# Two layers on one core: five PSUM banks for the exponentials behind the last maximum, and the second layer's routing steps placed later

## The reference, cut to what matters

```
x  = L0_attn_x                                  # (2, 1024, 128)
xn = layernorm(x);  s = attention(xn) @ WO;  g = silu(ffn0(xn));  x = x + s * g
xn = layernorm(x);  s = recurrent(xn);       g = silu(ffn1(xn));  x = x + s * g

attention:  score = Q K^T / sqrt(8) + causal mask;  exp(score - max) / sum;  times V
ffn1:       logits = x @ router_w;  raw = softmax(logits)
            idx1 = argmax(raw);  idx2 = argmax(raw without idx1)
            place of a token in its expert = exclusive count of the tokens before it in the group
            combine/dispatch by one-hot(place) ... expert -> gelu(x w0) * (x w1) -> wo
```

## Time and profile before

| | |
|---|---|
| median of three runs | 617.03 us |
| profiled execution, its own time | 616.33 us |
| its span, first to last instruction | 614.5 us |
| PE busy | 573.1 us (93%) |
| DVE busy | 476.7 us (78%) |
| ACT busy | 330.9 us (54%) |
| POOL busy | 190.4 us (31%) |
| mean granted TensorE clock | 0.981 |

### The profile page before, as it was taken

How to read it: one execution, slowest core, us unless ns; L and a number is a source line. 1 busy time by engine, 2 the same in 40 slices (tenths; PEclk the granted TensorE clock), 3 DMA queues, 4 the chain that set the end, 5 groups by cost and what they waited for, 6 DMA issues and landing times.

```text
span 614.5 us, 11961 instructions
## 1 busy us (share of the span) xinstructions
PE 573.1 (93%) x3901; PEld 352.2 (57%) x3902; DVE 476.7 (78%) x1307; ACT 330.9 (54%) x602; POOL 190.4 (31%) x221
## 2 busy tenths in 40 slices
PE   2878999999999999899999998989899999999996
PEld 1433544444444534899999963535446665656554
DVE  6799889999989898455555578666899899976465
ACT  2762567676777776555555558864223642362224
POOL 1451000000254452133333310000007685688300
PEclk9898899999999999999999999999999999999999
DMA  8955727070813171211111034215011322421412
GB/s 185 210 182 206 241 77 216 3 217 1 224 31 109 53 226 20 56 49 47 47 47 47 26 97 128 71 41 151 0 46 25 97 59 54 130 79 40 126 42 68
DMA packets 55612, 57.99 MB, mean 94 GB/s; under 512 B 8651, under 2 KB 39403, under 8 KB 55515
## 3 DMA queue, kind: packets, MB, share of 16 engines
q1 hardware_dynamic: 51242, 50.56, 29.9%
q0 software_dynamic: 4320, 6.81, 3.5%
HBM read 41.96 MB, written 18.85 MB: 99 GB/s over the span
## 4 chain that ended last, share of the span: by engine, by line
PE 76%; DVE 16%; ACT 4%; issue 2%; DMA 1%; SPq 1%; ACTq 0%; DVEq 0%
PE banks L1689 11%; PE banks L1831 10%; PE banks L1756 8%; PE banks L1778 7%; PE banks L1964 7%; PE banks L1701 6%; PE banks L1953 5%; PE banks L1950 5%; PE banks L2015 4%; DVE banks L1239 4%; DVE mpart L1242 3%; PE banks L1759 2%; ACT arena L809 1%; PE banks L1840 1%; PE banks L1598 1%
## 5 line engine op out<-in xcount | busy, mean ns | idle before, releaser
L809 ACT ACTIVATE arena<-banks 128x512 f32<-128x512 f32 (+1 forms) x304 | 154.3, 583 | 75.1 <-PE banks L1759 40.7
L1239 DVE CUSTOM_DVE_ANT_0 banks<-banks,arena 128x512 f32<-128x512 f32 (+3 forms) x256 | 119.7, 511 | 9.2 <-PE banks L1778 8.3
L1756 PE MATMUL banks<-arena 128*128 128x512 bf16 (+3 forms) x384 | 116.6, 331 | 4.0 <-ACT arena L809 2.8
L1778 PE MATMUL banks<-arena 96*128 96x512 bf16 (+3 forms) x384 | 113.5, 336 | 4.8 <-DVE mpart L1239 2.7
L1242 DVE TENSOR_REDUCE mpart<-banks 128x1 f32<-128x512 f32 x128 | 85.8, 683 | 9.1 <-PE banks L1778 8.1
L1689 PE MATMUL banks<-arena 128*128 128x128 f32 x624 | 76.3, 275 | 1.0 <-ACT arena L743 1.0
L1689 PEld LDWEIGHTS banks<-arena 128*128 128x128 f32 x624 | 72.8, 192 | 1.5 <-ACT arena L743 1.5
L1831 PE MATMUL banks<-arena 128*9 128x512 f32 (+3 forms) x768 | 70.7, 487 | 0.0
L851 ACT ACTIVATE arena<-banks 125x512 f32<-125x512 f32 (+2 forms) x48 | 28.4, 595 | 71.2 <-PE banks L1950 46.2
L1756 PEld LDWEIGHTS banks<-arena 128*128 128x128 bf16 x384 | 37.8, 99 | 49.6 <-issue 23.8
L620 POOL DMA_INDIRECT results<-arena x39 | 37.7, 967 | 77.4 <-DVE arena L1133 77.4
(11 more groups left out here) (295 smaller groups left out, 858.0 us busy)
## 6 DMA issues: line engine op xcount, KB each, us to landing
k_parts<-arena SPq DMA_DIRECT2D x6, 768.0 KB, 8.1
arena<-in_L_ffn_experts_w_dram SPq DMA_DIRECT2D x2, 2048.0 KB, 11.1
arena<-results SPq DMA_DIRECT2D x8, 512.0 KB, 6.6
arena<-k_parts SPq DMA_DIRECT2D x7, 576.0 KB
arena<-q_parts SPq DMA_DIRECT2D x28, 144.0 KB
arena<-in_L_ffn_w_kernel_dram SPq DMA_DIRECT2D x8, 344.0 KB, 3.8
slots<-in_pad_rows_dram SPq DMA_DIRECT2D x1, 2535.0 KB, 12.3
arena<-slots SPq DMA_DIRECT2D x39, 65.0 KB, 1.8
```

Of the source, the lines that this page charges most:

```text
L809: act.activation(Pr[:, r % 4, heads[0]:heads[-1] + 1, 0:n], ring_e[e % 3][:, 0:len(heads) * n].rearrange("p (j c) -> p j c", j=len(heads)) ...
L1239: ins = dve.tensor_tensor_reduce(unmasked, unmasked, tail_mask[:, 512 - n:512], 1.0, -BIG, ALU.add, ALU.max, part[:, at:at + 1])
L1756: ins = pe.matmul(ring_e[e % 3][:, at * n:at * n + n], QK[:, slot, j, 1, P * kt:P * kt + P], QK[:, slot, j, 0, q:q + n], start=True, stop= ...
L1778: ins = pe.matmul(ps[:, at * n:at * n + n], QK[0:TALL, slot, j, 0, P * i:P * i + P], QK[0:TALL, slot, j, 1, 512 * half:512 * half + n], st ...
```

## The change

Two things change, both for group 7 and the end of group 6.

First, from the last maximum on (it is the unit of group 7's head 3, tile 5, in group 6) the seven ring banks are dealt out anew: 0, 1, 2, 5 and 6 to the exponentials, 3 and 4 to the small units. A function that walks the step list takes for each step the bank used longest ago among those allowed, and notes which semaphore count says that the bank's last content has been read. The engines then wait for that count.

Second, `MIDDLE` puts the steps of layer 1 later: the two `x_turn` from keys 39 and 41 to 48 and 50, `logits1` and `route_max` from 45 and 46 to 54, `route_exp` and `scale` from 49 to 53, `route_choice` from 50 to 54, `places1` and `route_places` from 56 and 57 to 64.

```diff
-          28: [("norm", 0)], 30: [("norm", 1)], 39: [("x_turn", 0)], 41: [("x_turn", 1)], 45: [("logits1",)], 46: [("route_max",)], 49: [("route_exp",), ("scale",)], 50: [("route_choice",)], 56: [("places1",)], 57: [("route_places",)]}
+          28: [("norm", 0)], 30: [("norm", 1)], 48: [("x_turn", 0)], 50: [("x_turn", 1)], 53: [("route_exp",), ("scale",)],
+          54: [("logits1",), ("route_max",), ("route_choice",)], 64: [("places1",), ("route_places",)]}
...
+E_BANKS, M_BANKS = (0, 1, 2), (3, 4, 5, 6)
+E_BANKS_LAST, M_BANKS_LAST = (0, 1, 2, 5, 6), (3, 4)
...
+    last_maximum = max(n for n, step in enumerate(steps) if step[0] == "p1")
+    def take(banks, n, freed):
+        bank = min(banks, key=lambda i: (used[i], i))
+        before, used[bank], held[bank] = held[bank], n, freed
+        return bank, before
+    for n, step in enumerate(steps):
+        e_banks, m_banks = (E_BANKS, M_BANKS) if n < last_maximum else (E_BANKS_LAST, M_BANKS_LAST)
...
             def unit_free():
-                if unit >= 4:
-                    name, n = FREES[unit - 4]
+                if M_AFTER[unit] is not None:
+                    name, n = M_AFTER[unit]
                     pe.wait_ge(Z[name], n)
-                return ring_m[unit % 4]
+                return banks[:, M_BANK[unit], :]
...
-                        if e >= 3:
-                            pe.wait_ge(Z["e_free"], e - 2)
+                        if E_AFTER[e] is not None:
+                            name, freed = E_AFTER[e]
+                            pe.wait_ge(Z[name], freed)
```

More of the change, by code:

```diff
@@ L211 @@
 RING_STEPS = ("p1", "logits", "counts", "maxrow", "turn", "attn_turn", "attn_out", "x_turn", "places1", "logits1")
+E_BANKS, M_BANKS = (0, 1, 2), (3, 4, 5, 6)
+E_BANKS_LAST, M_BANKS_LAST = (0, 1, 2, 5, 6), (3, 4)
 def ring_tables():
     frees, unit_of, reads_before, reads = [], {}, {}, 0
[L218 to L221, removed]
+    e_bank, e_after, m_bank, m_after = [], [], [], []
+    steps = [step for k in range(-1, NG + 1) for step in PLANS[k]]
+    last_maximum = max(n for n, step in enumerate(steps) if step[0] == "p1")
+    used, held = dict.fromkeys(E_BANKS + M_BANKS, -1), dict.fromkeys(E_BANKS + M_BANKS)
+    def take(banks, n, freed):
[4 more added lines that the diff above has]
+        e_banks, m_banks = (E_BANKS, M_BANKS) if n < last_maximum else (E_BANKS_LAST, M_BANKS_LAST)
+        if step[0] == "exp":
+            bank, before = take(e_banks, n, ("e_free", len(e_bank) + 1))
+            e_bank.append(bank)
+            e_after.append(before)
+        elif step[0] in RING_STEPS:
+            unit_of[step] = len(frees)
             if step[0] == "maxrow":
                 frees.append(("mrow_ready", 2 * step[1] + step[2] + 1))
-            elif step[0] in RING_STEPS:
+            else:
                 reads += 1
                 frees.append(("m_free", reads))
[L227 to L232, removed]
+            bank, before = take(m_banks, n, frees[-1])
+            m_bank.append(bank)
+            m_after.append(before)
+        elif step[0] in ("negmax", "experts0"):
+            reads_before[step] = reads
+    return frees, unit_of, reads_before, reads, e_bank, e_after, m_bank, m_after
+FREES, UNIT_OF, READS_BEFORE, READS, E_BANK, E_AFTER, M_BANK, M_AFTER = ring_tables()
 def build(nc, x, WQ, WK, WV, WO, gate, w1, w2, w3, WomT, b_om, log_scale, gamma, beta, W1T, b1, W2T, b2,
@@ L358, in build @@
         psO = banks[:, 6:8, :].rearrange("p a c -> p (a c)")
-        ring_e = [banks[:, i, :] for i in range(3)]
-        ring_m = [banks[:, 3 + i, :] for i in range(4)]
         O = banks[:, 7, :]
@@ L800, in _ @@
                             act.wait_ge(mrow_in[half], 16 * (g - 1))
-                        act.copy(mrow[0:3 * HG, g % 2, 512 * half:512 * half + 512], ring_m[unit % 4][0:3 * HG, :]).then_inc(Z["mrow_ready"], 1)
+                        act.copy(mrow[0:3 * HG, g % 2, 512 * half:512 * half + 512], banks[0:3 * HG, M_BANK[unit], :]).then_inc(Z["mrow_ready"], 1)
                     elif step[0] == "exp":
@@ L809, in _ @@
                         act.activation(Pr[:, r % 4, heads[0]:heads[-1] + 1, 0:n],
-                                       ring_e[e % 3][:, 0:len(heads) * n].rearrange("p (j c) -> p j c", j=len(heads)), ACT.Exp,
+                                       banks[:, E_BANK[e], 0:len(heads) * n].rearrange("p (j c) -> p j c", j=len(heads)), ACT.Exp,
                                        scale=SCALE).then_inc(Z["e_free"], 1)
@@ L1752, in _ @@
                             pe.wait_ge(mrow_in[half], 16 * (k + 1))
-                        if e >= 3:
-                            pe.wait_ge(Z["e_free"], e - 2)
+                        if E_AFTER[e] is not None:
+                            name, freed = E_AFTER[e]
+                            pe.wait_ge(Z[name], freed)
                         for at, j in enumerate(heads):
-                            ins = pe.matmul(ring_e[e % 3][:, at * n:at * n + n], QK[:, slot, j, 1, P * kt:P * kt + P],
+                            ins = pe.matmul(banks[:, E_BANK[e], at * n:at * n + n], QK[:, slot, j, 1, P * kt:P * kt + P],
                                             QK[:, slot, j, 0, q:q + n], start=True, stop=kt // 4 != half)
                             if kt // 4 == half:
-                                ins = pe.matmul(ring_e[e % 3][:, at * n:at * n + P], upper_b, ident_b, start=False, stop=True)
+                                ins = pe.matmul(banks[:, E_BANK[e], at * n:at * n + P], upper_b, ident_b, start=False, stop=True)
                         ins.then_inc(Z["e_ready"], 1)
```

## The result

The changed kernel took 619.31 us (median of ten runs, 616.95 to 621.93), the kernel before 617.1 us (median of ten, 614.8 to 619.24). The ratio is 1.0046, with a 95% interval of 1.0029 to 1.0063: slower by 2.8 us (1.8 to 3.9), and clear of noise; the two medians lie 2.2 apart. The forecast was 617.4 with a range up to 618.9; the measured 619.31 lies outside. The profiled execution has a span of 617.4 us against 614.5.

The account below looks back on a forecast made before the run. Bound: PE (76% of the span), through the chain behind group 7's last division. Counts at 406.6 + 0.43 + 1.39 + 4.63 + 0.64 = 413.7 against 413.23, a loss of 0.5 us: 617.4 against the median of 617.03, range 615.0 to 618.9.

Parts of the forecast that it names:

- The walk through group 7: Step-by-step timing of PE, ACT and DVE in group 7: logits at 399.4, counts 406.6, 3.4 us later than before.
- ACT's stall: ACT at route_exp, now ahead of its own input, stands about 2 us; five banks cover part of it.
- The held division: Last half's division on DVE queues behind the one-hot blocks, using up 2.69 us of slack; PE's L1890 at 413.7.
- the way from the counts to DVE's L1227: On DVE's tail, 0.43 us from the counts' start on PE to L1208, 0.1 of it for the handover.
- The later of the two counts: End of group 7: DVE's tail at 413.7, later than PE's 412.0, sets L1890; loss 0.5 us against 413.23.
- both ends of TensorE's wait: Before L1890: PE's own tail would reach it at 412.0, DVE's division lets it start at 413.7.
- the prediction's own signs of being wrong: DVE idle ahead of L1309, PE idle over 1 us at stage 9, or a difference arising outside 384 to 414 us.
- C: ACT's stall at route_exp is not covered, late logits and counts: loss of 2.5 us, 619.5; chance 0.14.
- A: PE's tail sets the end, counts at 405.1 or earlier: gain 1.0 us on average, 616.0; chance 0.22.
- B: All of ACT's 6.5 us idle time in group 7 goes: 610.5; chance 0.04.
- D: New banks wait for reads of maxima and the switch itself stalls PE: 617.0; chance 0.02.

Follow-up runs that it names:

- making the wait in the kernel before: Kernel before with redundant one-hot writes on DVE ahead of the four blocks: ratio 1.0012 with three writes, 1.0076 with five.
- the table alone: Kernel before, its banks kept, with the changed kernel's step table (`MIDDLE`): ratio to the kernel before 1.0102 (1.0066 to 1.0137).
- the split kernel: Changed kernel with two of the four one-hot blocks moved behind the last division: ratio to the kernel before 0.9991 (0.9967 to 1.0016).
- the banks alone: Changed kernel's banks with the step table (`MIDDLE`) of the kernel before: ratio to the kernel before 0.9979 (0.9954 to 1.0005).

## Why the prediction was wrong, point by point

**The walk through group 7 held.** Forecast and measured: pv 0 and 1 at 389.42 (389.38), logits at 399.4 (399.42), DVE's copy at 401.3 (401.30), route_choice at 402.3 (402.36), 9/0 at 403.0 (402.96), counts at 406.6 (406.71), first transpose at 413.7 (413.84). ACT's stall was 2.08 for 2.0.

**The held division held too.** DVE's slack of 2.69 us was used up and the division followed the blocks without a pause. Splitting the blocks showed that this queue and nothing else held it: T1 moved by 1.72 us (29.29 to 27.57). The one small miss here is the way from the counts to DVE's L1227 (L1208 before): 0.53 us (406.71 to 407.24) in place of 0.43.

**The failed step is the one behind the walk:** "The later of the two counts: 413.7 against 413.23, a loss of 0.5 us." It took the lateness of the first transpose for the loss. I had worked out both ends of TensorE's wait, 412.0 and 413.7, but gave a price only to the difference from before, not to the 1.7 us of additional idleness, and let the matmuls behind it keep the durations of before. They ran at half the clock: 1.74 us between the first transpose and the output's addition, and a further 0.6 at the dispatch matmuls, where PE now came last. 0.5 + 1.7 + 0.6 = 2.8, the trace's 2.87 without the 0.09 before group 7; the times give 2.8 (1.8 to 3.9) and, repeated, 1.9 (0.1 to 3.6). Keeping TensorE busy left the 0.5 of lateness in the trace and took the 1.7 back; making the wait in the kernel before brought the same 4.83 us. One of the prediction's own signs of being wrong came true: 2.3 of the 2.8 us arise behind 414 us, where it had no step.

**The rivals.** C gave 619.5, nearly the measured time, but that is luck, for its reason was another: it wanted the logits at 400.2 and PE over 1 us idle at stage 9, and the trace shows 399.42 and 0.59. With the table alone and three banks its mechanism did come about: PE waits 1.14 us for ACT, and the start is 3.3 late where C had 2.5. None of A, B and D happened; A's end (PE's tail sets it) is what the split kernel has. That the clock could fall was no rival at all, and it should have been one: the prediction's own numbers had TensorE's wait before the transposes grow from 0.68 to 2.4 us.

## What to carry to other kernels

Where a step moves from a place with slack to one ahead of a result that the bound engine waits for, work out how long that engine will idle, and price what runs behind the wait at the lower clock too: here 0.5 us of lateness cost 2.8. When a ring is made deeper, look at which step the engine it frees will wait for next (with the banks alone, 1.38 us for the choice on DVE), and move or split that in the same edit: the same banks gave +0.46% with four blocks ahead of the division and -0.43% with two and a table that fits them.

## What the runs showed of the hardware that was not expected

The clock fell to 0.50 at the end of a wait of 2.40 us which followed the four matmuls of the turn and another wait of 0.71. Behind 1.68 us after the same four, it fell as well, but only during the output matmuls (granted 0.55 over them); behind 0.68 us it did not fall. In the run with the later route_exp the same wait of 2.40 us was followed by transposes at full speed, so one and the same wait can bring the fall about 2 us earlier or later. Each kernel but the two repeated ones has one trace, so how often it comes at which place isn't known:

```profile
414.81 1.09 PE L1909 MATMUL banks<-C,shared 128*128 128x128 f32 x8 [2.40 <-DVE shared L1310]
416.63 3.58 PE L1915 MATMUL banks<-arena 128*128 128x128 f32 x16 [0.72 <-ACT arena L854]
```
